# Gather stage of a fused attention and nearest-neighbour kernel: the weighting moved from GpSimd to VectorE, fp32 matmuls and spreads dealt out over the one-hot groups

## What is computed

```python
B, N, C, K = (8, 1024, 64, 30)     # as drawn; the kernel runs 32 batches, 1024 points, 128 channels
att = jax.nn.softmax(h[..., 0], axis=-1)          # weight of each of the 30 neighbours
xk = x.transpose(0, 2, 1)[bidx, idx]              # the neighbours' vectors
agg = jnp.einsum('bnkc,bnk->bnc', xk, att)
return x + agg.transpose(0, 2, 1)
```

## Time and profile before

| | value |
|---|---|
| median of three runs | 7002.95 us |
| profiled execution | 7007.53 us |
| its span | 7005.7 us |
| first `attend` matmul of the gather stage | 5677.6 us from the span's start |
| last `add` of the stage | 7002.5 us |
| one iteration of the loop (four quads) | 83.3 us |
| granted TensorE clock in the single iterations | 0.87 to 0.93 |

### The profile page before, as it was taken

How to read it: one execution, slowest core, us unless ns; L and a number is a source line. 1 busy time by engine, 2 the same in 40 slices (tenths; PEclk the granted TensorE clock), 3 DMA queues, 4 the chain that set the end, 5 groups by cost and what they waited for, 6 DMA issues and landing times. The chain is left out here.

```text
span 7005.7 us, 167053 instructions
## 1 busy us (share of the span) xinstructions
PE 4995.6 (71%) x63824; PEld 2914.5 (42%) x63824; DVE 5607.1 (80%) x6966; ACT 4002.8 (57%) x8974; POOL 2816.6 (40%) x3300
## 2 busy tenths in 40 slices
PE   6887878878878787788877878872000058888888
PEld 3444444444444444444444444441000046666666
DVE  8877877877778777787877778764789888888887
ACT  4666655666666656565655656564222256666666
POOL 2444444544445444444444454441000034444443
PEclk8788878788878877888788788775555579998989
DMA  1000000000000000000000000000000000000000
GB/s 37 13 14 14 14 23 16 13 14 14 14 26 14 14 13 14 25 14 14 13 14 14 25 14 14 13 10 1 0 0 0 0 20 27 31 27 28 27 27 27
DMA packets 35795, 114.00 MB, mean 16 GB/s; under 512 B 5488, under 2 KB 6128, under 8 KB 34800
## 3 DMA queue, kind: packets, MB, share of 16 engines
q1 hardware_dynamic: 34928, 102.28, 4.1%
HBM read 68.71 MB, written 33.55 MB: 15 GB/s over the span
## 5 line engine op out<-in xcount | busy, mean ns | idle before, releaser
L550 ACT ACTIVATE ohT<-oh_ps,cst 128x512 bf16<-128x512 f32 x1920 | 1277.4, 691 | 389.1 <-PE oh_ps L430 384.0
L448 PE MATMUL g_ps<-tparts,ohT 128*128 128x24 bf16 x23040 | 921.7, 178 | 795.9 <-ACT ohT L550 785.5
L448 PEld LDWEIGHTS g_ps<-tparts,ohT 128*128 128x128 bf16 x23040 | 765.7, 100 | 1439.3 <-ACT ohT L550 1335.8
L794 DVE MAX8 vals<-pd_sb 128x8 f32<-128x1024 f32 x1024 | 1205.3, 1213 | 134.2 <-ACT pd_sb L550 112.5
L799 DVE FIND_INDEX8 idx<-vals,pd_sb 128x8 uint16<-128x1024 f32 x1024 | 1244.2, 1218 | 0.0
L801 DVE MATCH_REPLACE8 pd_sb<-vals,pd_sb 128x1024 f32<-128x1024 f32 x768 | 927.8, 1208 | 0.0
L430 PE MATMUL oh_ps<-bitsT,code 128*128 128x512 bf16 x1920 | 875.2, 461 | 2.2 <-ACT bitsT L707 2.2
L550 ACT ACTIVATE pd_sb<-pd_ps,nxx 128x512 f32<-128x512 f32 x512 | 355.1, 694 | 863.9 <-PE pd_ps L354 862.5
L818 DVE TENSOR_REDUCE mx<-s_ps 128x8 f32<-128x512 f32 x256 | 176.4, 689 | 722.0 <-PE s_ps L389 722.0
L1560 POOL TENSOR_TENSOR e_wgt<-e_hot,e_pairs 120x1024 bf16<-120x1024 bf16 x192 | 478.4, 2516 | 660.7 <-DVE e_hot L1603 660.7
L1681 PE MATMUL e_a_ps<-planes,e_oh 120*128 120x32 bf16 x24576 | 673.5, 179 | 92.9 <-DVE e_oh L1636 53.9
(11 more groups left out here) (200 smaller groups left out, 7519.0 us busy)
## 6 DMA issues: line engine op xcount, KB each, us to landing
ctx_s<-in_ctx SPq DMA_DIRECT2D x32, 512.0 KB, 4.3
maskb<-in_mask_Bx1x_ff SPq DMA_DIRECT2D x32, 512.0 KB, 5.1
x_s<-in_x SPq DMA_DIRECT2D x32, 512.0 KB, 5.8
y_spill<-y_s SPq DMA_DIRECT2D x32, 512.0 KB, 2.9
e_y<-y_spill SPq DMA_DIRECT2D x32, 512.0 KB, 3.7
out<-e_o SPq DMA_DIRECT2D x64, 256.0 KB, 2.0
pd_sb<-in_shape_constants SPq DMA_DIRECT2D x1, 1024.0 KB, 5.0
cst<-in_shape_constants SPq DMA_DIRECT2D x1, 242.5 KB, 2.7
```

The costliest lines, as they stand in the source:

```text
L448: m = nc.tensor.matmul(g_ps[:, k % GK, t, :], ohT[:, k % 2, bass.ts(t, P)], tparts[:, par, part, :], start=(part == 0), stop=(part == PART ...
L550: return nc.scalar.activation(dst, src, func, scale=scale, bias=bias)
L794: nc.vector.max(vals[:, i, :], pd_sb[:, (t + i) % RING, :]).then_inc(topk_step, 1)
```

## The change

- `weigh` goes from GpSimd to VectorE. VectorE runs one of its three instructions behind each of the groups 2, 3 and 4. GpSimd keeps `norm` and `rows` alone.
- VectorE's eight spreads are dealt out two by two behind groups 4 to 7, ScalarE's four spreads one by one behind groups 3 to 6.
- `heat` goes from behind group 2 to behind group 1.
- `gathered` is dealt out: its first two of eight matmuls behind group 1, and one each behind groups 2 to 7. Its result is complete at the end of the quad and not early in it.
- So `add` goes from behind group 5 to behind group 0 of the quad that follows. One more `add` stands behind the loop.
- `normalise` goes behind group 2, `turn_rows` behind group 5, `turned_rows` behind group 7.

No instruction of work is added or taken away.

```diff
@@ scalar
-            def spread(n, q):
+            def spread(n, q, t):
                 act.wait_ge(weighted, n * PARTS + 1)
-                for t in range(QT):
-                    m = a.activation(spr[q][pp, 0, t], wgt[pp, 0], ACT.Copy, scale=con["tmask"][pp, t:t + 1])
-                m.then_inc(spread_first, 1)
+                m = a.activation(spr[q][pp, 0, t], wgt[pp, 0], ACT.Copy, scale=con["tmask"][pp, t:t + 1])
+                if t == QT - 1:
+                    m.then_inc(spread_first, 1)
...
                         moved(n, q, g)
-                        if g == 1 and ahead:
-                            spread(n + 1, 1 - q)
-                        if g == 3 and q == QUADS - 1 and not last:
+                        if g in (3, 4, 5, 6) and ahead:
+                            spread(n + 1, 1 - q, g - 3)
+                        if g == 2 and q == QUADS - 1 and not last:
+                            normalise(b + 1, j if par == 0 else j + 1, 1 - par)
+                        if g == 7 and q == QUADS - 1 and not last:
                             turned_rows(b + 1, 1 - par)
@@ gpsimd
-                for q in range(QUADS):
-                    if not (last and q == QUADS - 1):
-                        weigh(b * QUADS + q + 1, 1 - q)
-                    if q == 0 and not last:
-                        norm(b + 1)
-                        rows(b + 1)
+                if not last:
+                    norm(b + 1)
+                    rows(b + 1)
@@ vector
-            def spread(n, q, part):
+            def weigh(n, q, part):
+
+                if part == 0:
+                    dve.wait_ge(hot_ready, n + 1)
+                    if passed(n):
+                        dve.wait_ge(spread_first, n)
+                elif passed(n):
+                    dve.wait_ge(spread_last, n * (PARTS - 1) - (PARTS - 1) + part)
+                att = pairs_s[pp, q, DIGITS + part, :].rearrange("p (n o d) -> p n o d", o=1, d=2)
+                v.tensor_tensor(wgt[pp, part], hot[pp], att.to_broadcast([QCOLS, P // 2, HI, 2]), ALU.mult).then_inc(weighted, 1)
+
+            def spread(n, q, part, rows):
...
-                        if g in (4, 5) and not (last and q == QUADS - 1):
-                            spread(n + 1, 1 - q, g - 3)
-                        if g == 5 and passed(n):
-                            add(n - 1, b if q == 1 else b - 1, 1 - q, par if q == 1 else 1 - par)
-                        if g == 2 and not (last and q == QUADS - 1):
+                        if g == 0 and passed(n - 1):
+                            add(n - 2, b - 1, q, 1 - par)
+                        if last and q == QUADS - 1:
+                            continue
+                        if g == 1:
                             heat(n + 1, 1 - q)
+                        if g in (2, 3, 4):
+                            weigh(n + 1, 1 - q, g - 2)
+                        if g >= 4:
+                            spread(n + 1, 1 - q, 1 + (g - 4) // 2, ((0, 1), (2, 3))[g % 2])
@@ tensor
+            parts_after = {1: (0, 1), 2: (2,), 3: (3,), 4: (4,), 5: (5,), 6: (6,), 7: (7,)}
...
                         attend(n, q, g)
-                        if g == 1:
-                            if passed(n):
-                                gathered(n - 1, 1 - q, b if q == 1 else b - 1, par if q == 1 else 1 - par)
-                            if q == QUADS - 1 and not last:
-                                turn_rows(b + 1, 1 - par)
+                        if g in parts_after and passed(n):
+                            gathered(n - 1, 1 - q, b if q == 1 else b - 1, par if q == 1 else 1 - par, parts_after[g])
+                        if g == 5 and q == QUADS - 1 and not last:
+                            turn_rows(b + 1, 1 - par)
```

More of the change, by code:

```diff
@@ L1519, in _ @@
             turned_rows(0, 0)
-            spread(0, 0)
+            for t in range(QT):
+                spread(0, 0, t)
             batches(act, emit)
@@ L1572, in _ @@
             rows(0)
-            weigh(0, 0)
             batches(pool, emit)
@@ L1598, in heat @@
                 dve.wait_ge(pairs_ready, n + 1)
-                if passed(n):
-                    dve.wait_ge(weighted, n * PARTS)
                 high = pairs_s[pp, q, 1, :].rearrange("p (n o d) -> p n o d", o=1, d=2)
@@ L1605, in heat @@
                                 ALU.is_equal).then_inc(hot_ready, 1)
-            def spread(n, q, part):
+            def weigh(n, q, part):
[8 more added lines that the diff above has]
+            def spread(n, q, part, rows):
                 dve.wait_ge(weighted, n * PARTS + part + 1)
-                for t in range(QT):
+                for t in rows:
                     m = v.tensor_scalar(spr[q][pp, part, t], wgt[pp, part], con["tmask"][pp, t:t + 1], None, ALU.mult)
-                m.then_inc(spread_last, 1)
+                if rows[-1] == QT - 1:
+                    m.then_inc(spread_last, 1)
             def add(n, b, q, par):
@@ L1637, in emit @@
                                         row.to_broadcast([QCOLS, NB // 2, LO, 2]), ALU.is_equal).then_inc(oh_ready, 1)
-                        if g in (4, 5) and not (last and q == QUADS - 1):
-                            spread(n + 1, 1 - q, g - 3)
-                        if g == 5 and passed(n):
-                            add(n - 1, b if q == 1 else b - 1, 1 - q, par if q == 1 else 1 - par)
-                        if g == 2 and not (last and q == QUADS - 1):
+                        if g == 0 and passed(n - 1):
[3 more added lines that the diff above has]
+                        if g == 1:
                             heat(n + 1, 1 - q)
+                        if g in (2, 3, 4):
+                            weigh(n + 1, 1 - q, g - 2)
+                        if g >= 4:
+                            spread(n + 1, 1 - q, 1 + (g - 4) // 2, ((0, 1), (2, 3))[g % 2])
             cut(0)
             heat(0, 0)
+            for part in range(PARTS):
+                weigh(0, 0, part)
             for part in range(1, PARTS):
-                spread(0, 0, part)
+                spread(0, 0, part, range(QT))
             batches(dve, emit)
+            add(B * QUADS - 2, B - 1, 0, 1)
             add(B * QUADS - 1, B - 1, 1, 1)
@@ L1684, in attend, with gathered @@
                 m.then_inc(a_ready, 1)
-            def gathered(n, q, b, par):
-                pe.wait_ge(a_moved, (n + 1) * NGR)
-                pe.wait_ge(xT_ready, b + 1)
-                if passed(n - 1):
-                    pe.wait_ge(o_added, n - 1)
-                for e in range(HI):
+            def gathered(n, q, b, par, part):
+                if part[0] == 0:
+                    pe.wait_ge(a_moved, (n + 1) * NGR)
+                    pe.wait_ge(xT_ready, b + 1)
+                    if passed(n - 1):
+                        pe.wait_ge(o_added, n - 1)
+                for e in part:
                     m = nc.tensor.matmul(o_ps[q][:], xT[:, par, e, :], at[:, q, e].rearrange("p t n -> p (t n)"),
                                          start=(e == 0), stop=(e == HI - 1))
-                m.then_inc(o_ready, 1)
+                if part[-1] == HI - 1:
+                    m.then_inc(o_ready, 1)
+            parts_after = {1: (0, 1), 2: (2,), 3: (3,), 4: (4,), 5: (5,), 6: (6,), 7: (7,)}
             def emit(b, j, par, last):
@@ L1717, in _ @@
             batches(pe, emit)
-            gathered(B * QUADS - 1, 1, B - 1, 1)
+            gathered(B * QUADS - 1, 1, B - 1, 1, range(HI))
 _INS = ['x', 'ctx_4096', 'mask_Bx1x4096_ff1', 'L0_xattn_W_in', 'L0_xattn_b_in', 'L0_xattn_W_out', 'L0_xattn_b_out',
```

8 lines of the change are left out of this document (removed).

## The result

| | before | after |
|---|---|---|
| median of four runs on one chip | 7005.85 us | 6926.4 us (6919.2 to 6930.9) |
| ratio, with 95% interval | 1 | 0.9884 [0.9866, 0.9901] |
| profiled execution, its span | 7007.53, 7005.7 us | 6927.13, 6925.3 us |
| gather stage, first turned-rows matmul to last gathered one | 1339.2 us (5663.3 to 7002.5) | 1254.7 us (5667.4 to 6922.0) |
| one loop iteration | 83.3 us (13 of them) | 78.1 us (12 of them) |

What follows compares the result with a forecast made beforehand. The prediction took TensorE as what the chain needs next, with a floor of 70.3 us in an iteration of 83.3. Its terms summed to -29.7 us, giving 6973 us on the median; own range 6945 to 6989, eight in ten 6915 to 7018.

Steps and rivals of the forecast that it cites:

- waits for VectorE: TensorE's waits for a one-hot in the gather stage go, since VectorE's load per quad falls below TensorE's: -41.4 us.
- waits for ScalarE: TensorE's waits for ScalarE's copy, in every second quad, go as the turned-rows copy moves behind group 7: -13.3 us.
- stage's beginning: At the gather stage's start, faster first weightings save about 3.5 us and a shorter first quad 4.5: together -8 us.
- unnamed waits: Waits amid attend matmuls without a shown releaser, 12.0 us, shrink as fp32 matmuls stand between groups: -6 us, bounds 0 and 12.
- blocks: Entering and leaving a gathered block costs 0.09 us; six more in each of 63 quads: +34 us, bounds 0 and 72.
- new wait by the add: At group 1, TensorE waits 0.5 us for a one-hot behind the add, in 50 quads: +25 us, bounds 0 and 30.
- the jump: TensorE's idle time where the loop jumps back stays at 61 us; load beside it adds 0, bounds 0 and 22.
- matmuls at the lower clock: In the loop iterations, slower work at the lower clock, 41 us, comes back by half: -20 us, bounds 0 and 41.
- The clock does not come back: Rival, chance 0.17: the new wait at each quad's border keeps the clock oscillating; 6993 us, no measurable change.
- switching is dear: Rival, chance 0.12: TensorE's changes between bf16 and fp32 cost 0.30 us per block, not 0.09; 7052 us.
- The load at the jump: Rival, chance 0.05: the next batch's load, now beside the jump, delays it; +20 us on the forecast, 6993.
- the gain is whole: Rival, chance 0.15: clock and unnamed waits come back entirely and the new wait shrinks to 10 us; 6932 us.

Runs made afterwards that it cites:

- 6: Kernel after with the add behind group 1 and the gathered matmuls dealt out so that none stands behind group 7: 6905.4 us.
- 9: Kernel after with the add behind group 1 and the gathered matmuls dealt out so that three stand behind group 7: 6871.8 us.
- 12: Kernel before with the weighting on VectorE, gathered as one block behind group 7, and the add behind group 1 of the next quad: 7145.7 us.
- Experiment 4: Kernel before with the load of the next batch issued behind the store of the second half: 7005.7 us.
- kernel 13: Kernel after with the add behind group 1, the load behind the store of the second half, and all batches written out without a loop: 6824.3 us.
- experiment 2: Kernel after with the weighting alone put back on GpSimd, everything dealt out staying so: 7044.6 us.
- Experiment 11: Kernel before with the weighting on VectorE and three PSUM buffers for the attend matmuls in place of two: 6918.0 us.
- experiment 5: Kernel after with the add behind group 1 and the load of the next batch issued behind the store of the second half: 6871.6 us.
- 7: Kernel after with the add behind group 1 and four batches in a loop's body, 7 iterations: 6855.7 us.
- 3: Kernel after with the add behind group 1 in place of group 0: 6892.4 us.

## Why the prediction came out as it did

Term by term over the stage, in us. The rows of waits leave some of the time out, so the last column is worked out from the traces of before and after step by step: from the start of each of the stage's 26,176 matmul records to the start of the next, less what the same step takes undisturbed at the upper clock (25 ns after an attend record, 429 after a gathered one, 109 after one of `turn_rows`, 56 after one of `turn_pairs`). The undisturbed steps are the same 1099.2 us in both kernels. What is left is put to the wait that stands there, to the lower clock where the clock was at its lower level, or to a slow row.

| step | predicted | before | after | measured |
|---|---|---|---|---|
| waits for VectorE | -41.4 | 45.8 | 0 | -45.8 |
| waits for ScalarE | -13.3 | 19.0 | 0.3 | -18.7 |
| stage's beginning (waits up to 5700 us) | -8 | 21.1 | 12.8 | -8.3 |
| unnamed waits | -6 | 14.9 | 10.7 | -4.2 |
| blocks | +34 | 3.5 | 35.4 | +31.9 |
| new wait by the add (49 of the 51, those behind 5700 us) | +25 | 0 | 31.5 | +31.5 |
| the jump | 0 | 63.3 | 34.5 | -28.8 |
| slow rows of attend matmuls at the upper clock | not in the sum | 23.2 | 6.1 | -17.1 |
| matmuls at the lower clock | -20 | 46.8 | 22.7 | -24.1 |
| rest | 0 | | | -0.9 |
| sum | -30 | | | -84.5 |

**The step that failed** is "The jump. It stays at 61 us." It measured 28.6 us less (32.4), 28.8 start to start, more than half of what the sum missed (55). The step bounded the jump by what the load could add and took 0; a gain was not within the bounds. The earlier trace rows shows an idle of 4.52 behind attend matmuls, and the forecast took it for the jump's whole length. It is the jump less what was queued ahead of it, and the change altered what is queued there: experiments 6, 9 and 12 show that the idle time follows the tail down to nothing. Experiment 4 gives 0.5 of the 2.15 us per jump to the load. The exact split of the rest stays open: after's tail is 0.94 us, and kernel 6, with no fp32 matmul at the end, already has 3.68, where kernel 4 has 4.13. What TensorE waits for at a jump no row shows; kernel 13, without the loop, doesn't have the wait.

**The clock** was about right in size: 24 us against 20. The reading ahead of it was not. It gave TensorE's whole remainder of 3.7 us per iteration to the lower clock; in the 13 iterations the lower clock cost 2.9, slow rows of attend matmuls 1.5, and 0.9 was hidden at the waits. (The floor of 70.3 held 0.76 of the slow rows already, so these terms don't add up to 3.7.) The lower level costs little in an attend matmul (27 ns from start to start in place of 25) and much in an fp32 record (815 in place of 429). That the clock rose is measured (0.90 to 0.97 in the 800 us), and experiment 2 shows that the dealing out does it even beside 106.6 us of waits: matmuls at the lower clock cost 25 us there, and 47 in before. "The clock does not come back", a rival at 0.17, fell. The new waits of 0.5 us at each quad's border left the clock at 1.00 in the 61 us above, and the 0.50 window of the earlier trace rows holds attend matmuls alone, in rows that the change has broken up. The prediction had this rival as a rule of the Trainium skill ("TensorE: Matmul & The Clock Gate", A second HAM failure mode: psum-queue depth-cycling). What the Trainium skill describes in that section is another kernel, in which frequent short idles between matmul groups made the clock swing. The traces of after (1.00 in the 61 us with three such waits) and of kernel 2 (0.97 with 156) don't agree with it as a rule.

**What the sum left out.** First, the waits' full length. A wait's row begins where the last record ends, 0.15 us too late; in before that hides 4.4 us at the waits for VectorE and as much at those for ScalarE. Second, the slow rows, 17 us. The 5.04 us for 192 attend matmuls, read as their pace, held 0.19 of ScalarE's: after's groups, one by one, take 4 x 1.21 = 4.85. Longer rows lose more. Experiment 11 shows that two buffers are the cause.

**Right, by its own steps.** The blocks (0.083 against 0.09), so "switching is dear" fell; the stage's beginning; VectorE nearly unstretched and not the bound (1.26 us per one-hot and 16.2 us busy per quad, against 1.21 and 15.4); ScalarE level with TensorE; the wait by the add, at its place and of its length in the row (0.49), though its true cost was 0.64 and the term's bad end 30. The load at the jump was a rival of 0.05 and is partly there: unnamed waits of 8.9 us, and some 16 us in all by experiment 5, more than compensated by the tail. The nearest of the cases was "the gain is whole" (6932). It came near by luck: its new wait of 10 us was 33 (51 x 0.64), its clock of 41 was 24, its unnamed waits of 12 were 4, and the jump and the slow rows, which it left alone, made up for that. Without the jump and the slow rows (46 us) the stage would have gained 39 us, close to the 30 of the sum. That the time with them still fell into the wide range is luck too, for neither stood in its terms as a gain.

**Parts.** Of the gain, 68 us come with the weighting alone. The dealing out alone loses 39 us, in waits for a stretched VectorE; on top of the weighting it gains 11, and 45 with the add one group later.

## What to carry to other kernels

Weigh a loop's jump as a whole, with its idle time, the waits and the clock behind it (5 us here, not 2.4), and ask what is queued ahead of it: a change that puts long matmuls there, or takes them away, changes the jump. Take costs from start to start: idle rows are short by the last record's tail, and a row without idle time can still be held back by its buffers. And an instruction that waits for a result should stand a group behind the point where the result comes, not right behind it.

## What the runs showed of the chip that was not expected

- The idle time of TensorE at a jump was 4.64, 3.68, 2.42, 1.39 and 0 us, by the matmuls ahead of it; without any jump the stage became 48 us shorter (kernel 13 against 5), and half the jumps gave 35 (7 against 3).
- The granted clock was 0.97 with 156 waits of 0.7 us, where fp32 matmuls stood between the groups, and 0.80 in kernel 12, whose waits lay between groups of attend matmuls.
- A bf16 multiply of 120 x 1024 took 2.52 us on GpSimd and 0.77 on VectorE. Beside it VectorE's own instructions had been stretched by more than the multiply costs there: VectorE's busy time fell by 90 us when it took the work over.
- At the lower clock a bf16 attend matmul cost 27 ns in place of 25, an fp32 record 815 in place of 429: where the lower clock falls decides what it costs.
